# A recommendation tower on one core: squares summed from PSUM in quads, with columns turned in runs of four per batch row

## The reference

```python
def _L0_rec_ref(embeds, inner_w):
    delta = jnp.einsum('uf,bfe->bue', inner_w, embeds)
    lp = jnp.sum(delta * delta, axis=-1)
    return lp
e = jnp.stack([tbl_0[ids[:, 0]], tbl_1[ids[:, 1]], ...], axis=1)   # (2048, 39, 64)
z = _L0_rec_ref(e, L0_rec_inner_w)                                 # (2048, 128)
h = jnp.concatenate([z, dense_ctx], axis=1)
h = jnp.maximum(h @ W_top1 + b_top1, 0.0)    # 144 -> 512
h = jnp.maximum(h @ W_top2 + b_top2, 0.0)    # 512 -> 256
y = h @ W_top3                               # 256 -> 1
```

## Time and profile before

| | |
|---|---|
| median of 3 runs | 570.52 us (567.47 to 572.12) |
| the profiled execution | 569.8 us |
| its span | 568.1 us |
| PE, POOL, DVE, ACT busy | 445.9, 412.0, 440.6, 224.3 us |
| mean granted TensorE clock | 0.916 of full speed |
| DMA | 100.43 MB, mean 177 GB/s |

### The profile page before, as it was taken

One profiled execution on the slowest core, in us unless ns is written; L12 is line 12 of the kernel. 1 busy time (PEld: TensorE's weight loads), 2 busy tenths in 40 slices (PEclk: granted clock), 3 DMA queues, 4 the chain that ended last, 5 costly groups with the idle time before them and its releaser, 6 DMA issues.

```text
span 568.1 us, 10177 instructions
## 1 busy us (share of the span) xinstructions
PE 445.9 (78%) x3376; PEld 388.9 (68%) x3376; DVE 440.6 (78%) x716; ACT 224.3 (39%) x312; POOL 412.0 (73%) x343
## 2 busy tenths in 40 slices
PE   0556869887799769968999879967998799865566
PEld 0556858786688659857878668856987698744334
DVE  2899759898689967868988967868989998854631
ACT  2543124243244433423533433443544444443432
POOL 6888778778777778778887878778887887872000
PEclk9997999899899888988999889988999999966677
DMA  6773477667776666748776666747766886474510
GB/s 174 211 198 88 116 213 228 201 176 191 187 210 191 192 165 172 212 111 222 207 197 188 192 177 177 211 123 223 213 203 171 227 218 187 129 214 123 183 50 1
DMA packets 67594, 100.43 MB, mean 177 GB/s; under 512 B 15750, under 2 KB 22554, under 8 KB 67548
## 3 DMA queue, kind: packets, MB, share of 16 engines
q1 hardware_dynamic: 56696, 88.61, 52.1%
q0 software_dynamic: 10752, 11.03, 10.3%
q10 hardware_dynamic: 100, 0.16, 0.1%
HBM read 36.31 MB, written 0.16 MB: 64 GB/s over the span
## 4 chain that ended last, share of the span: by engine, by line
POOL 72%; issue 19%; PE 4%; DMA 2%; SPq 1%; ACT 1%; DVE 1%; POOLq 0%; ACTq 0%
POOL x_all L389 72%; PE side L456 2%; PE side L448 1%; SPq L338 1%; PE delta L489 1%; DMA xs<-xl 1%; ACT sq_all L557 1%; DMA x_all<-tbl,idx 0%; DMA dense_f<-dense_t 0%; PE side L461 0%; PE turned L475 0%; DVE z L668 0%; DMA idx<-ids 0%; SPq L347 0%; ACT h L566 0%
## 5 line engine op out<-in xcount | busy, mean ns | idle before, releaser
L389 POOL DMA_INDIRECT x_all<-tbl,idx x336 | 411.3, 1224 | 103.6 <-issue 101.8
L431 PE MATMUL side<-table,onehot 125*128 125x192 bf16 x2496 | 245.2, 259 | 43.8 <-DVE table L718 19.1
L431 PEld LDWEIGHTS side<-table,onehot 125*128 125x128 bf16 x2496 | 218.1, 104 | 68.7 <-issue 48.8
L489 PE MATMUL delta<-xs,ws 117*128 117x512 f32 (+1 forms) x272 | 121.8, 488 | 63.2 <-DMA xs<-xl 48.5
L664 DVE TENSOR_TENSOR acc_all<-acc_all,sq_all 128x1024 f32<-128x1024 f32 x112 | 136.5, 1219 | 18.3 <-ACT sq_all L557 17.3
L541 ACT ACTIVATE xh<-turned 117x512 fp32r<-117x512 f32 x96 | 54.0, 562 | 208.4 <-PE turned L475 201.2
L637 DVE TENSOR_SCALAR onehot<-idh,row_no 125x1024 bf16<-125x1024 f16 x312 | 130.1, 481 | 6.9 <-DMA idh<-ids 6.9
L656 DVE TENSOR_REDUCE x_all<-side 128x128 f32<-128x384 f32 x144 | 77.0, 551 | 64.2 <-PE side L431 63.2
L557 ACT ACTIVATE sq_all<-delta 128x1024 f32<-128x1024 f32 x112 | 112.4, 1022 | 28.9 <-PE delta L489 27.9
L489 PEld LDWEIGHTS delta<-xs,ws 117*128 117x128 f32 x272 | 52.4, 211 | 82.6 <-DMA xs<-xl 41.5
L475 PEld LDWEIGHTS turned<-ident,x_all 128*117 128x117 f32 x352 | 86.3, 310 | 9.3 <-DMA x_all<-tbl,idx 6.1
(11 more groups left out here) (30 smaller groups left out, 80.5 us busy)
## 6 DMA issues: line engine op xcount, KB each, us to landing
xs<-xh SPq DMA_DIRECT2D x160, 234.0 KB
xs<-xl SPq DMA_DIRECT2D x80, 234.0 KB
idh<-ids SPq DMA_DIRECT2D x72, 224.0 KB
x_all<-tbl,idx POOLq DMA_INDIRECT x336
xs<-xh SPq DMA_DIRECT2D x32, 117.0 KB
x_all<-tbl SPq DMA_DIRECT2D x12, 224.0 KB
idh<-ids SPq DMA_DIRECT2D x72, 26.0 KB
xs<-xl SPq DMA_DIRECT2D x16, 117.0 KB
```

Of the source, the lines that this page charges most:

```text
L389: pool.indirect_dma_start(x_slots[k][:, f, 0:E], None, tables[f], bass.IndirectOffsetOnAxis(idx[k][:, f:f + 1], 0),).then_inc(gathered[k], 16)
L431: mm = pe.matmul(side[n % 2][:, q * PARTS * E:(q + 1) * PARTS * E], onehot[k % OHR][:, c, q, h * TB:(h + 1) * TB], table[k][:, q, c, :, :] ...
L489: mm = pe.matmul(delta[quad % 2][:, c:c + cols], ws[:, :], xs[i % XS][:, j, 0:SIZE[u], :].rearrange("p g b -> p (g b)"), start=True, stop= ...
```

## The change

- `turned` and with it `xh`, `xl` and `xs` hold a unit's columns with the batch row outside and the turned column inside (b g), where it was (g b): each transpose now writes its 128 results four elements apart (two in the last unit), and the other readers and writers of these tiles take them flat.
- `project` writes a `delta` bank in the same order; the two matmuls of the last `n` write their 256 results in runs of two.
- `square` writes its result over its input, in PSUM; `sq` is gone.
- `add` becomes a reduction: for each quad, quad 0 too, VectorE sums the 8 squares of each batch row out of `delta` into one column of `z_part` (SBUF, 128 rows by 8 quads). After the last quad it reduces `z_part` over the quads into `z`.
- `project` waits for `summed` where it waited for `squared`.
- The two tiles of indices that lay in `sq_all` at the start lie in `z_part`.

The cut diff:

```diff
-        xh = sb("xh", [KT, XR, G, TB], F32R)
+        xh = sb("xh", [KT, XR, TB * G], F32R)
-        sq_all = sb("sq_all", [P, SQ, 4 * NB], F32)
-        acc_all = sb("acc_all", [P, 2, 4 * NB], F32)
+        z_part = sb("z_part", [P, TB, QUADS], F32)
...
     def transpose(s, h, u, p):
+                    rows = turned[u % 2][0:KT, 0:SIZE[u] * TB].rearrange("p (b g) -> p b g", g=SIZE[u])
                     for g in range(SIZE[u]):
                         e0 = G * u + g
-                        mm = pe.transpose(turned[u % 2][0:KT, g, :], x[2 * p + h][:, e0:e0 + EG * (KT - 1) + 1:EG], ident[:, :])
+                        mm = pe.transpose(rows[:, :, g], x[2 * p + h][:, e0:e0 + EG * (KT - 1) + 1:EG], ident[:, :])
...
     def project(s, h, n):
                     if n % 2 == 0:
-                        wait(pe, squared, at_quads(s, h) + quad - 1)
-                    cols = SIZE[u] * TB
+                        wait(pe, summed, at_sums(s, h) + quad - 1)
+                    size = SIZE[u]
+                    bank = delta[quad % 2][:, (n % 2) * 2 * NB:(n % 2 + 1) * 2 * NB].rearrange("p (b g) -> p b g", g=G)
                     for m, j in enumerate(js):
-                        c = (n % 2) * 2 * NB + m * cols
-                        mm = pe.matmul(delta[quad % 2][:, c:c + cols], ws[:, :],
-                                       xs[i % XS][:, j, 0:SIZE[u], :].rearrange("p g b -> p (g b)"), start=True, stop=True)
+                        mm = pe.matmul(bank[:, :, m * size:(m + 1) * size], ws[:, :],
+                                       xs[i % XS][:, j, 0:size * TB].rearrange("p (b g) -> p b g", g=size), start=True, stop=True)
...
     def square(s, h, quad):
                     act.wait_ge(projected, at_quads(s, h) + quad + 1)
-                    if quad == 0:
-                        to = acc[h]
-                    else:
-                        wait(act, summed, at_sums(s, h) + quad - 1 - (SQ - 1))
-                        to = sq[(h * (QUADS - 1) + quad - 1) % SQ]
-                    act.activation(to[:, :], delta[quad % 2][:, :], ACT.Square).then_inc(squared, 1)
+                    act.activation(delta[quad % 2][:, :], delta[quad % 2][:, :], ACT.Square).then_inc(squared, 1)
...
     def add(s, h, quad, p):
-                    if quad == 0:
-                        return
                     dve.wait_ge(squared, at_quads(s, h) + quad + 1)
-                    if quad > 1:
-                        dve.wait_ge(summed, at_sums(s, h) + quad - 1)
-                    dve.tensor_tensor(acc[h][:, :], acc[h][:, :], sq[(h * (QUADS - 1) + quad - 1) % SQ][:, :], ALU.add).then_inc(summed, 1)
+                    if quad == 0:
+                        wait(dve, z_ready, s * SIDES + h)
+                    dve.tensor_reduce(z_part[:, :, quad], delta[quad % 2][:, :].rearrange("p (k b g) -> p b k g", b=TB, g=G),
+                                      AX.XY, ALU.add).then_inc(summed, 1)
                     if quad == QUADS - 1:
-                        dve.wait_ge(summed, at_sums(s, h) + quad)
-                        dve.tensor_reduce(z[p][:, h * TB:(h + 1) * TB], acc[h][:, :].rearrange("p (e b) -> p b e", b=TB), AX.X,
-                                          ALU.add).then_inc(z_ready, 1)
+                        dve.wait_ge(summed, at_sums(s, h) + QUADS)
+                        dve.tensor_reduce(z[p][:, h * TB:(h + 1) * TB], z_part[:, :, :], AX.X, ALU.add).then_inc(z_ready, 1)
```

More of the change, by code:

```diff
@@ L65 @@
 MOVES = 3
-SQ = 2
 OHR = 3
@@ L163, in build @@
         row_no = {ch: sb(f"row_no{ch}", [KP, ch], F32) for ch in sorted(set(PAIR_CH))}
-        xh = sb("xh", [KT, XR, G, TB], F32R)
-        xl = sb("xl", [KT, XR, G, TB], F32R)
-        xs = [sb(f"xs{k}", [3 * F, J, G, TB], F32R) for k in range(XS)]
+        xh = sb("xh", [KT, XR, TB * G], F32R)
+        xl = sb("xl", [KT, XR, TB * G], F32R)
+        xs = [sb(f"xs{k}", [3 * F, J, TB * G], F32R) for k in range(XS)]
         ws = sb("ws", [3 * F, U], F32R)
         ident = sb("ident", [P, P], F32)
-        sq_all = sb("sq_all", [P, SQ, 4 * NB], F32)
-        sq = [sq_all[:, k, :] for k in range(SQ)]
-        ids_all = sq_all[0:PAIRS * STEPS, 0, 0:2 * NB].bitcast(I32)
-        ids_low = sq_all[0:PAIRS * STEPS, 1, 0:DUP * NB].bitcast(F16).rearrange("p (d c) -> p d c", d=DUP)
-        acc_all = sb("acc_all", [P, 2, 4 * NB], F32)
-        acc = [acc_all[:, k, :] for k in range(2)]
+        z_part = sb("z_part", [P, TB, QUADS], F32)
+        ids_all = z_part[0:PAIRS * STEPS, 0:TB // 2, :].rearrange("p b e -> p (b e)").bitcast(I32)
+        ids_low = z_part[0:PAIRS * STEPS, TB // 2:TB, :].rearrange("p b e -> p (b e)").bitcast(F16).rearrange("p (d c) -> p d c", d=DUP)
         z = [sb(f"z{k}", [P, NB], F32) for k in range(2)]
@@ L194, in build @@
         delta = [pb(f"delta{k}", [P, 4 * NB], F32) for k in range(2)]
-        turned = [pb(f"turned{k}", [P, G, TB], F32) for k in range(2)]
+        turned = [pb(f"turned{k}", [P, TB * G], F32) for k in range(2)]
         side = [pb(f"side{k}", [P, 512], F32) for k in range(2)]
@@ L245, in build @@
         at_quads = lambda s, h: s * (SIDES * QUADS) + h * QUADS
-        at_sums = lambda s, h: s * (SIDES * (QUADS - 1)) + h * (QUADS - 1)
+        at_sums = lambda s, h: s * (SIDES * QUADS) + h * QUADS
         at_looks = lambda s: (s + 1) * LOOKS
@@ L337, in restack @@
                         for c in copies:
-                            sp.dma_start(to[c:3 * F:3, :, 0:size, :].rearrange("p j g b -> p j (g b)").bitcast(F32),
-                                         half[:, i % XR, 0:size, :].rearrange("p g b -> p (g b)").bitcast(F32)).then_inc(stacked[i % XS], 16)
+                            sp.dma_start(to[c:3 * F:3, :, 0:size * TB].bitcast(F32), half[:, i % XR, 0:size * TB].bitcast(F32)).then_inc(stacked[i % XS], 16)
                 def load_dense(s):
@@ L540, in high_half @@
                         act.wait_ge(stacked[last % XS], at_stack(then, last))
-                    act.activation(xh[:, i % XR, 0:SIZE[u], :], turned[u % 2][0:KT, 0:SIZE[u], :], ACT.Copy).then_inc(xh_ready, 1)
+                    act.activation(xh[:, i % XR, 0:SIZE[u] * TB], turned[u % 2][0:KT, 0:SIZE[u] * TB], ACT.Copy).then_inc(xh_ready, 1)
                 def dense_half(s):
@@ L643, in low_half @@
                     i = h * UNITS + u
-                    dve.tensor_tensor(xl[:, i % XR, 0:SIZE[u], :], turned[u % 2][0:KT, 0:SIZE[u], :],
-                                      xh[:, i % XR, 0:SIZE[u], :].bitcast(F32), ALU.subtract).then_inc(xl_ready, 1)
+                    dve.tensor_tensor(xl[:, i % XR, 0:SIZE[u] * TB], turned[u % 2][0:KT, 0:SIZE[u] * TB],
+                                      xh[:, i % XR, 0:SIZE[u] * TB].bitcast(F32), ALU.subtract).then_inc(xl_ready, 1)
                 def dense_rest(s):
@@ L658, in add @@
                 def add(s, h, quad, p):
+                    dve.wait_ge(squared, at_quads(s, h) + quad + 1)
                     if quad == 0:
-                        return
-                    dve.wait_ge(squared, at_quads(s, h) + quad + 1)
-                    if quad > 1:
-                        dve.wait_ge(summed, at_sums(s, h) + quad - 1)
-                    dve.tensor_tensor(acc[h][:, :], acc[h][:, :], sq[(h * (QUADS - 1) + quad - 1) % SQ][:, :], ALU.add).then_inc(summed, 1)
+                        wait(dve, z_ready, s * SIDES + h)
+                    dve.tensor_reduce(z_part[:, :, quad], delta[quad % 2][:, :].rearrange("p (k b g) -> p b k g", b=TB, g=G),
+                                      AX.XY, ALU.add).then_inc(summed, 1)
                     if quad == QUADS - 1:
-                        dve.wait_ge(summed, at_sums(s, h) + quad)
-                        dve.tensor_reduce(z[p][:, h * TB:(h + 1) * TB], acc[h][:, :].rearrange("p (e b) -> p b e", b=TB), AX.X,
-                                          ALU.add).then_inc(z_ready, 1)
+                        dve.wait_ge(summed, at_sums(s, h) + QUADS)
+                        dve.tensor_reduce(z[p][:, h * TB:(h + 1) * TB], z_part[:, :, :], AX.X, ALU.add).then_inc(z_ready, 1)
                 def rows(s):
```

## The result

| | before | changed |
|---|---|---|
| median (all runs) | 569.0 us (565.93 to 572.12, 4 runs) | 583.15 us (579.7 to 586.11, 4 runs) |
| ratio | | 1.0246, 95% interval 1.0162 to 1.033 |
| profiled execution, span | 569.8, 568.1 us | 586.11, 584.4 us |

A forecast was written before the change was run, and what follows sets the result against it. GpSimd's gathers were taken to pace the kernel. From the profiled span, 568.1 - 34.4 (gathers) + 17.6 (held bank) + 4 (VectorE) - 0.7 (small terms) = 554.6, plus 1.7 outside the span: forecast 556 us, range 538 to 590.

The forecast's parts named there:

- What bounds the kernel: GpSimd's gathers pace everything, through SyncE's index loads and the restacks behind them; gathers hold 72% of the chain of waits.
- Why the gathers are slow: GpSimd's gathers are stretched by 72 us, mainly while VectorE runs an add reading two SBUF tensors, also under one-hot builds.
- Term 1: GpSimd's gathers: sums reading PSUM remove 52 of 72 us of stretch, bringing -34.4 us.
- term 3: VectorE's work: reductions of 1.22 us each add 8.4 us in all, half put on the path, +4 us.
- small terms: Shorter last side, -0.7 us; ScalarE's square into PSUM at 1.02 us and stepped column turns at 0.22 us taken as unchanged.
- the wait of 5.7: TensorE's one wait for GpSimd, 5.7 us at the last half, was to go.
- The floor of 56.85 us: Pace of steps 5 and 6, taken for steps 1 to 4 too: 227.4 instead of 256.1 us, -28.7.
- Term 2: PSUM bank held until VectorE's sum: TensorE starts quads later, +17.6 us, half of the upper bound of 35.3.
- The count of late starts: In the old trace TensorE began 57 of 126 quads before VectorE's add of the quad two before ended, by 44.8 us.
- (b): Rival: none of TensorE's bank delay is hidden, or GpSimd is relieved less: 578 us; chance 0.19 for 566 and above.
- (c): Rival: VectorE's reduction out of PSUM costs what the z reduction L668 does, 1.92 us: 603 us; chance 0.14.
- (d): Rival: stepped PSUM writes of TensorE's column turns cost double, 9.7 us more a step: 585 us; chance 0.10.

The follow-up runs named there:

- e8_fewer: The kernel before with 17 of the 21 gathers of each side, the four other fields zero: 542.34 us, ratio 0.9534.
- e1: The changed kernel with the squares back in SBUF and TensorE waiting for the square, not the sum: 546.26 us, ratio 0.9605 against the kernel before.
- f3: e1 with one wait changed: TensorE takes a delta buffer again when it has been summed, not squared: 583.38 us, ratio 1.0263 against the kernel before.
- e2_hold: The kernel before with one wait more, TensorE waiting for VectorE's add of the quad two before: 580.6 us, ratio 1.0212.
- e4: The kernel before with the new layout alone, squares and adds in SBUF as they were: 567.84 us, ratio 0.9976.
- f5: e1 in the old layout, so that sums read 8 squares 512 bytes apart from SBUF: 593.44 us, ratio 1.0472 against the kernel before.

## Why the prediction was wrong

- **What bounds the kernel** (GpSimd, and through the index loads everything): right for the kernel before. e8_fewer leaves gathers out, and gains 26 us.
- **Why the gathers are slow** (the `add` with two SBUF inputs): right, 72 us of stretch became 16, where 20 was worked out. By what means an `add` slows a gather no run shows; that a one-input sum relieves it, from SBUF as from PSUM, e1 shows.
- **Term 1, -34.4 us: right in kind, a third too large.** e1_sq_sbuf gives 545.0 - 568.1 = -23.1 of span, term 3 and the small terms within it, for which together -31.1 was forecast. The end came out as taken or better (8.3 us less where the wait of 5.7 was to go); steps 1 to 4 lost 16.0 where 28.7 was taken. The floor of 56.85 us came from steps 5 and 6, which contain no loop return; in e1 steps 1 and 3 come to 58.0 and 59.4, 2 and 4 only to 60.8 and 61.9.
- **Term 2, +17.6 us: the step that failed.** It is 37.1 us by f3 against e1, twice what was taken and about the upper bound of 35.3 (the runs of the two spread by 3 to 5 us, so 37.1 can't be told from it). The count of late starts was sound: on e1's trace it gives 61 of 126 quads, by 43.0 us, where the old trace gave 57 and 44.8. What failed was its price. Half was taken for want of a reason, and the term held only lateness, as if TensorE's busy time stayed the same at any amount of waiting. By the two profiles, TensorE's idle time grew by 17.6 us, and its busy time, at a granted clock of 0.900 for 0.931, by 20.1, a cost that stands nowhere in the prediction. That 17.6 is also the number taken is luck; nothing in the halving leads there. The count also leaves the `add`s where they stood, while a late TensorE makes ScalarE's square late and with it the sum that TensorE waits for next; how much that adds isn't measured.
- **Terms 1 and 2 don't add.** The sum took relief and hold as independent. e2_hold has the hold without relief and takes 580.6, the changed kernel has both and takes 583.2: within the spread of their runs the relief is worth nothing once the bank loop paces the steps. The hold costs 12.5 us with slow gathers and 37.1 with fast ones.
- **Term 3**: 1218 ns for the 1.22 forecast; the reductions aren't the bound. Its 4 us weren't isolated.
- **Small terms**: turns unchanged (e4), the square in place 1012 ns (1022 before), both as taken.
- **Rivals**: (b), "nothing of the delay is hidden", at 578, comes nearest, but in its number only: two thirds of the 61 us of new waits stand where others were, and what it lacks is TensorE's longer busy time. (c), a slow reduction, doesn't happen out of PSUM, but f5 shows the very case: 1927 ns a sum and 593 us. (d), the turns' stepped writes: the rule that, with PSUM's 8-byte cachelines, any non-contiguous pattern slows matmuls significantly (Trainium skill, PSUM — Partial Sum Buffer, Specifications) doesn't show here: these fp32 turns, which write 4 bytes of every 16, take 368 ns as before. The 256-column matmuls, which write runs of 8 bytes, keep their 343 ns.

## What to carry to other kernels

A buffer that a tensor engine waits for should be freed by the first engine that reads it: two buffers shared by three engines in a row put both queues into the loop, and here that cost 37 us, to save a write into SBUF that cost nothing measurable. About half of it wasn't waiting but the same matmuls at a lower granted clock, so look at an engine's busy time too when it is made to wait. Before adding a gain and a loss, ask whether both would be paced by the same engine; a relief is worth nothing behind a new bound. The better kernel was one step away: sums with one input in place of `add`s with two (they are what frees GpSimd), runs of four (for SBUF's sake), squares in SBUF, and with nothing hanging on the sums, sums late in the queue: 540.8 us, 5.3% faster than before.

## What was not expected of the hardware

A reduction of 1024 elements takes 1.93 us if it reads SBUF 512 bytes apart and 1.22 us from PSUM with the same step. A return of the loop leaves TensorE without an instruction for 3.0 to 4.2 us, twice in each kernel here but f5_sbuf_old, whose trace shows one such gap, of 2.5 us. Holding a buffer longer, by one changed wait, lowered TensorE's mean granted clock from 0.931 to 0.900, and the same matmuls took 20 us longer.
